# Expert tiles of two halves of 128 rows, each half with its own pair of experts

## What is computed

```
mod = (silu(c) @ wmod)                      # per sequence: sa, ca, ga, sb, cb, gb (ga, gb kept away from 0)
h = layernorm(x) * (1 + ca) + sa
x = x + ga * scan(h)                        # h_t = a_t * h_(t-1) + (1 - a_t) * v_t, times a sigmoid gate
h = layernorm(x) * (1 + cb) + sb
probs = softmax(h @ gate_w.T + gate_b)      # 8 experts
topk_vals, topk_idx = top_k(probs, 2)
y_e = relu(h @ w1[e] + b1[e]) @ w2[e] + b2[e]          # 128 -> 512 -> 128
x = x + gb * (topk_vals[0] * y_(first) + topk_vals[1] * y_(second))
```

## Time and profile before

| | us |
|---|---|
| median of 3 runs (lowest, highest) | 469.36 (467.02, 471.52) |
| the profiled execution | 468.58 |
| its span, from first to last instruction | 466.8 |
| mean granted TensorE clock, share of full | 0.923 |
| first stage, until the table is written | 0 to about 177 |
| expert tiles, first transposition to the end | 181.8 to 466.8 |

### The profile page before, as it was taken

One profiled execution on the slowest core, in us unless ns is written; L12 is line 12 of the kernel. 1 busy time (PEld: TensorE's weight loads), 2 busy tenths in 40 slices (PEclk: granted clock), 3 DMA queues, 4 the chain that ended last, 5 costly groups with the idle time before them and its releaser, 6 DMA issues.

```text
span 466.8 us, 14531 instructions
## 1 busy us (share of the span) xinstructions
PE 400.2 (86%) x4122; PEld 334.3 (72%) x4123; DVE 416.6 (89%) x1159; ACT 300.1 (64%) x746; POOL 214.4 (46%) x225
## 2 busy tenths in 40 slices
PE   1958888799888843998999999999999999999960
PEld 1434656456656742897999999999999988888960
DVE  4899999998989998987998999999999999999970
ACT  1447998787995610775767676677777666666630
POOL 8023330674775778854443444433333443333331
PEclk9997999978987555999999999999999999999995
DMA  7615534544223335442332333333333333222210
GB/s 228 187 47 190 164 127 117 178 144 148 104 85 121 129 147 160 161 132 68 104 107 65 102 99 82 101 86 86 82 85 89 85 82 82 82 67 77 67 44 15
DMA packets 47258, 50.51 MB, mean 108 GB/s; under 512 B 5342, under 2 KB 40879, under 8 KB 47202
## 3 DMA queue, kind: packets, MB, share of 16 engines
q1 hardware_dynamic: 39152, 32.64, 24.8%
q0 software_dynamic: 6976, 16.93, 10.0%
q10 hardware_dynamic: 1074, 0.23, 0.2%
HBM read 26.90 MB, written 24.57 MB: 110 GB/s over the span
## 4 chain that ended last, share of the span: by engine, by line
PE 55%; DVE 17%; issue 10%; POOL 9%; ACT 3%; DMA 3%; POOLq 1%; SPq 0%; ACTq 0%; DVEq 0%
POOL sorted_rows L562 9%; PE bank L1502 7%; PE bank L1519 7%; PE bank L1520 7%; PE bank L1522 7%; PE bank L1503 7%; PE bank L1504 7%; PE bank L1368 4%; DVE xn L922 3%; PE bank L1514 2%; PE bank L1488 2%; DVE st L860 2%; DVE hs L936 2%; DVE st L866 2%; DVE u L932 2%
## 5 line engine op out<-in xcount | busy, mean ns | idle before, releaser
L592 POOL DMA_INDIRECT out_dram<-tg,midx x90 | 103.0, 1145 | 151.3 <-DVE tg L1297 129.4
L756 ACT ACTIVATE xs<-bank,b1col 128x256 f32<-128x256 f32 x360 | 136.9, 488 | 26.2 <-PE bank L1504 20.9
L1519 PE MATMUL bank<-w2hi,xs 128*128 x720 | 119.2, 219 | 0.0
L1520 PE MATMUL bank<-w2hi,w2f 128*128 x720 | 119.0, 219 | 0.0
L1278 DVE TENSOR_TENSOR w2f<-xs 128x1024 f16<-128x1024 f32 x90 | 110.3, 1226 | 3.1
L1502 PE MATMUL bank<-xh,w1hi 128*128 128x256 f16 x360 | 98.8, 274 | 1.9 <-DVE xl L1269 1.9
L1522 PE MATMUL bank<-w2lo,xs 128*128 x720 | 98.9, 219 | 0.0
L1503 PE MATMUL bank<-xl,w1hi 128*128 128x256 f16 x360 | 98.7, 274 | 0.0
L1504 PE MATMUL bank<-xh,w1lo 128*128 128x256 f16 x360 | 98.6, 274 | 0.0
L562 POOL DMA_INDIRECT sorted_rows<-pay,idx x64 | 72.7, 1137 | 30.9 <-issue 18.8
L1520 PEld LDWEIGHTS bank<-w2hi,w2f 128*128 128x128 f16 x720 | 70.5, 98 | 0.8
(11 more groups left out here) (232 smaller groups left out, 671.2 us busy)
## 6 DMA issues: line engine op xcount, KB each, us to landing
xs<-sorted_rows SPq DMA_DIRECT2D x45, 260.0 KB, 2.8
sorted_rows<-padt SPq DMA_DIRECT2D x10, 582.0 KB, 5.2
xs<-sorted_rows SPq DMA_DIRECT2D x45, 128.0 KB, 2.5
w2f<-in_L_ffn_w_dram SPq DMA_DIRECT2D x4, 512.0 KB, 3.6
xs<-in_L_ffn_w_dram SPq DMA_DIRECT2D x4, 512.0 KB, 4.0
xs<-in_L_attn_x_dram SPq DMA_DIRECT2D x3, 512.0 KB, 8.5
out_dram<-tg,midx POOLq DMA_INDIRECT x90, 3.0
sorted_rows<-pay,idx POOLq DMA_INDIRECT x64, 2.7
```

Of the source, the lines that this page charges most:

```text
L592: pool.indirect_dma_start(out_rows, bass.IndirectOffsetOnAxis(midx[k][:, t:t + 1], 0), yout[k][:, t, :], None, bounds_check=TOK - 1, oob_i ...
L756: ins = act.activation(hf[e][:, cc, :], bank[2 * e + cc // 2][:, (cc % 2) * TW:(cc % 2 + 1) * TW], ACT.Relu, bias=b1col[:, bass.ds(ex[e] * ...
L1519: pe.matmul(o[t], hh[n % 2][e][:, cc, t * P:(t + 1) * P], whi, start=False, stop=False)
L1520: pe.matmul(o[t], hl[n % 2][e][:, cc, t * P:(t + 1) * P], whi, start=False, stop=False)
```

## The change

A tile is still 256 rows in two halves, but each half (a unit of `UNIT` = 128 rows) now has its own pair of experts. A pair with n tokens takes units of 128 rows, rounded up, and two units that follow each other in the table make a tile, whatever their experts are. The code of a tile holds four experts. DVE makes it from two table entries (`both_codes`), and PE and ACT wait for `codes_ready`. Layer 1 now runs by half (128 columns moving), `hidden` has 16 activations of 128x128, the bias of layer 2 is one matmul of 128 columns for each half and expert, and SP issues two DMAs for x and two for y, each with its own row number. The four weight arrays are cut into 16 tensors (one for each chunk of 128 hidden values, all experts in each), so that all addresses of an expert are one product plus a constant each. `addresses` has them worked out eight at a time before the matmuls of a half (nine with the bias). The padding takes 5 DMAs in place of 10; `drop`, `kept` and `row_mid` are half as large. The loads of w1 have runs of 512 B where they had 2 KB. Cut to its core:

```diff
-SPAN = TOK + TW
+UNIT = P
+SPAN = TOK + UNIT
-MAX_TURNS = (TOK // TW + PAIRS) // BUFS
+MAX_TURNS = (TOK // UNIT + PAIRS + 1) // (BUFS * HALVES)
...
-        w1hi = sb("w1hi", [P, E * H], F16)
-        w1lo = sb("w1lo", [P, E * H], F16)
-        w2hi = sb("w2hi", [P, E * H], F16)
-        w2lo = sb("w2lo", [P, E * H], F16)
+        w1hi, w1lo, w2hi, w2lo = ([sb(f"{n}{cc}", [P, E * D], F16) for cc in range(HC)]
+                                  for n in ("w1hi", "w1lo", "w2hi", "w2lo"))
...
-            return [code % E, code // E]
+            return [[code % E, code // E % E], [code // E ** 2 % E, code // E ** 3]]
...
             def load_x(it, k):
-                sp.dma_start(xin[k][:, :, :], tile_rows(it, k)[:, :, 0:D]).then_inc(x_tile_in[k], 16)
+                for t in range(HALVES):
+                    sp.dma_start(xin[k][:, t, :], unit_rows(it, k, t)[:, 0:D]).then_inc(x_tile_in[k], 16)
...
             def hidden(it, n, ex):
...
-                    for cc in range(HC):
-                        ins = act.activation(hf[e][:, cc, :], bank[2 * e + cc // 2][:, (cc % 2) * TW:(cc % 2 + 1) * TW],
-                                             ACT.Relu, bias=b1col[:, bass.ds(ex[e] * HC + cc, 1)])
+                    for t in range(HALVES):
+                        for cc in range(HC):
+                            o = cc % 2 * TW + t * P
+                            ins = act.activation(hf[e][:, cc, t * P:(t + 1) * P], bank[2 * e + cc // 2][:, o:o + P],
+                                                 ACT.Relu, bias=b1col[:, bass.ds(ex[t][e] * HC + cc, 1)])
...
-                done1 = marked(dve.tensor_tensor(cnti[:, 0:1], tend[:, PAIRS - 1:PAIRS], early_end[:, PAIRS - 1:PAIRS], ALU.add))
+                done1 = marked(dve.scalar_tensor_tensor(out=cnti[:, 0:1], in0=tend[:, PAIRS - 1:PAIRS], scalar=1.0,
+                                                        in1=early_end[:, PAIRS - 1:PAIRS], op0=ALU.add, op1=ALU.add))
...
-                done1 = marked(dve.tensor_scalar(cntt[:, 0:1], cnti[:, 0:1], BUFS.bit_length() - 1, None,
+                done1 = marked(dve.tensor_scalar(cntt[:, 0:1], cnti[:, 0:1], (BUFS * HALVES).bit_length() - 1, None,
                                                  ALU.arith_shift_right))
...
+            dve.wait_ge(table_ready, 1)
+            dve.scalar_tensor_tensor(out=both_codes[:, :], in0=bank[6][0:4, 1:P:2], scalar=float(E * E),
+                                     in1=table[:, 0:P:2], op0=ALU.mult, op1=ALU.add).then_inc(codes_ready, 1)
...
+            def addresses(expert, loaded, streamed=()):
+
+                for w in loaded:
+                    pe.to_reg(expert * D * 2 + (nc.lookup_mloc(w).addr + (P - 1) * 2))
+                for w in streamed:
+                    pe.to_reg(expert * D * 2 + nc.lookup_mloc(w).addr)
...
-                    for cc in range(HC):
-                        o = bank[2 * e + cc // 2][:, (cc % 2) * TW:(cc % 2 + 1) * TW]
-                        whi, wlo = (w[:, bass.ds(ex[e] * H + cc * P, P)] for w in (w1hi, w1lo))
-                        pe.matmul(o, whi, xh[n % 2][:, :], start=True, stop=False)
-                        pe.matmul(o, whi, xl[n % 2][:, :], start=False, stop=False)
-                        ins = pe.matmul(o, wlo, xh[n % 2][:, :], start=False, stop=True)
+                    for t in range(HALVES):
+                        addresses(ex[t][e], w1hi + w1lo)
+                        rows = slice(t * P, (t + 1) * P)
+                        for cc in range(HC):
+                            o = bank[2 * e + cc // 2][:, cc % 2 * TW + t * P:cc % 2 * TW + (t + 1) * P]
+                            whi, wlo = (w[cc][:, bass.ds(ex[t][e] * D, P)] for w in (w1hi, w1lo))
+                            pe.matmul(o, whi, xh[n % 2][:, rows], start=True, stop=False)
+                            pe.matmul(o, whi, xl[n % 2][:, rows], start=False, stop=False)
+                            ins = pe.matmul(o, wlo, xh[n % 2][:, rows], start=False, stop=True)
...
+                    for t in range(HALVES):
+                        addresses(ex[t][e], (), [b2row] + w2hi + w2lo)
+                        o = y_bank(n)[:, e * TD + t * D:e * TD + (t + 1) * D]
+                        rows = slice(t * P, (t + 1) * P)
+                        pe.matmul(o, ones16[:, :], b2row[:, bass.ds(ex[t][e] * D, D)], start=True, stop=False)
+                        for cc in range(HC):
+                            whi, wlo = (w[cc][:, bass.ds(ex[t][e] * D, D)] for w in (w2hi, w2lo))
+                            pe.matmul(o, hh[n % 2][e][:, cc, rows], whi, start=False, stop=False)
+                            pe.matmul(o, hl[n % 2][e][:, cc, rows], whi, start=False, stop=False)
+                            ins = pe.matmul(o, hh[n % 2][e][:, cc, rows], wlo, start=False, stop=cc == HC - 1)
...
-            held = [pe.alloc_register(f"held_expert{i}") for i in range(4)]
+            held = [pe.alloc_register(f"held_expert{i}") for i in range(8)]
```

More of the change, by code:

```diff
@@ L444, in settled @@
             def settled(n):
-                sp.wait_ge(landed, sp.value_load(table[2:3, n:n + 1], min_val=1, max_val=2))
+                last = n * HALVES + HALVES - 1
+                sp.wait_ge(landed, sp.value_load(table[2:3, last:last + 1], min_val=1, max_val=2))
                 sp.sem_inc(sp_turn, 1)
@@ L747, in experts_of @@
             def experts_of(it, n):
-                code = act.value_load(table[1:2, bass.ds(it * BUFS + n, 1)], min_val=0, max_val=E * E - 1)
-                return experts(act, code)
+                return experts(act.value_load(both_codes[1:2, bass.ds(it * BUFS + n, 1)], min_val=0, max_val=E ** 4 - 1))
             def hidden(it, n, ex):
@@ L1245, in tile_table @@
                 dve.wait_ge(dve_step, done)
[L1246 removed]
+                done = marked(dve.scalar_tensor_tensor(out=full[:, :], in0=sums[:, 2:3], scalar=-float(UNIT), in1=place[:, :],
                                                        op0=ALU.add, op1=ALU.min))
[L1248 removed]
+                mark(dve.scalar_tensor_tensor(out=over[:, :], in0=place[:, :], scalar=UNIT - (UNIT - 1) / 2, in1=sums[:, 2:3],
                                               op0=ALU.add, op1=ALU.subtract))
@@ L1259, in _ @@
             join()
-            dve.tensor_scalar(kept[:, :, :], row_mid[:, :, :], sums[:, 4:5], over[:, 0:1], ALU.mult, ALU.is_lt
+            dve.tensor_scalar(kept[:, :], row_mid[:, :], sums[:, 4:5], over[:, 0:1], ALU.mult, ALU.is_lt
                               ).then_inc(drop_made, 1)
@@ L1524, in layer2 @@
                 ins.then_inc(yps_ready, 1)
-            held = [pe.alloc_register(f"held_expert{i}") for i in range(4)]
+            held = [pe.alloc_register(f"held_expert{i}") for i in range(8)]
             def hold(before, now):
-                for reg, value in zip(held, before + now):
+                for reg, value in zip(held, [v for ex in (before, now) for half in ex for v in half]):
                     pe.reg_mov(reg, value)
             def held_experts():
-                b0, b1_, n0, n1 = (pe.snap(reg, min_val=0, max_val=E - 1) for reg in held)
-                return [b0, b1_], [n0, n1]
+                v = [pe.snap(reg, min_val=0, max_val=E - 1) for reg in held]
+                return [v[0:2], v[2:4]], [v[4:6], v[6:8]]
```

105 lines of the change are left out of this document (46 added, 59 removed).

## The result

The changed kernel takes 450.13 us (median of four runs, 448.51 to 452.80) against 468.19 us (465.48 to 471.52) of the kernel before on the same chip. The ratio is 0.9639, 95% interval 0.9596 to 0.9682. Its profiled execution has a span of 448.0 us (before 466.8), so 18.8 us are to be accounted for.

A forecast was written before the change was run, and what follows sets the result against it. PE was taken to stream columns without a gap in written-out tiles, losing about 0.25 us a tile in the loop. -36.0 + 2.7 + 2.8 + 3.1 + 1.3 = -26.1 us gave 443 us, range 432 to 463.

The forecast's parts named there:

- The tiles: Expert stage: 39 tiles for 45, all six taken from the hardware loop at 6.00 us each, 36.0 us saved.
- The array: PE, layer 1: 48 matmuls of 128 columns, 5.79 us a tile, 0.05 more; as slower-than-before rival, chance 0.02.
- The sequencer: PE's register work: +2.7 us in written-out tiles, +2.8 in the loop; as pace-setting rival 453 to 463 us, chance 0.14.
- the hole of 0.1 us ahead of layer 2: PE, written-out tiles: an issue wait before layer 2's first weight load, 0.1 us lost for each tile.
- a little more than that lead: PE's sequencer: hole between the layers becomes about 1.1 us, against a lead of about 1.0 us in steady tiles.
- The bound on this term: PE's sequencer: batches half as dear again (0.45 us) give 6.3 to 6.5 us for every tile, up to +19 us.
- the foretold lack of lead: Hardware loop: PE's sequencer has no lead there, 6.4 against 6.00 us on 7 intervals, +2.8 us.
- ACT: Sixteen activations take 4.3 us, hidden under 5.79 a tile, +1.3 at the end; as pace-setting rival, chance 0.06.
- The start: First tiles: more DMA issues by SP ahead of the third tile's x, +3.1 us.
- x comes 5 us later, and 1.9 of them aren't lost: Third tile's x lands about 5 us later, avoiding PE's old 1.94 us wait behind DVE: 5.0 - 1.9 = +3.1 us.
- wait of DVE near 212: Sign to look for: DVE's 4 us wait for the first written tile, until 212.46 before, is gone.
- The end: Last tile: nothing covers the lateness of ACT's activations, +1.3 us.

The follow-up runs named there:

- two traces of kernels that don't split the DMAs: Kernel before with layer 1 as 48 matmuls of 128 columns (ratio 1.0080); kernel before with 16 activations of 128x128 for 8 of 128x256 (1.0034).
- the other traces with this start: Changed kernel with 20 or 128 small matmuls, 18 turns, no read in the loop, or wide activations: 42.2 to 43.3 us from first to eighth transposition.
- the kernels with split DMAs: Kernel before with each x and y load issued as two DMAs of 128 rows: 472.71 us against 467.64, ratio 1.0152.
- ACT's halves: Kernel before with ACT's 8 activations of 128x256 a tile made 16 of 128x128: 468.78 us, ratio 1.0034.
- the version with both mended: Changed kernel with y loads of the first two tiles issued later and 20 small matmuls ahead of the tiles: 441.73 us, ratio 0.9412.

## Why the prediction was right, and where it was not

It gave 443 us in a range of 432 to 463; 450.13 lies in it, 7 us above the value.

**The tiles: right.** 39 of them, x loads in 78 parts, six intervals of 6.00 us fewer. It was the whole gain, and it came from counting units in the data and taking the price from the place where the tiles go, the loop.

**The array: right.** 0.056 us for a matmul of 128 columns in layer 1 too; the splitting alone costs 0.06 us a tile where 0.05 was said. A whole tile, 100 of them with two transpositions, takes 5.835 us.

**The sequencer: the mechanism right, one place wrong.** The batches are two packed instructions each, and taking them away costs 3.5 us a tile. But the hole of 0.1 us ahead of layer 2 in written-out tiles isn't there: "a little more than that lead" was a difference of two numbers about 1 us each. The interval grew by 0.09 all the same (5.745 to 5.835, steady), 0.06 from the split of layer 1, and 0.03 that no run here takes apart. So +2.3 for +2.7 is partly luck. The bound on this term was also added up too low: with batches half as dear again, eight of them put 1.2 us on the 5.1 to 6.0, which is up to 7.2 us a tile and not 6.5. It didn't come to that. In the loop the foretold lack of lead is what happens: the gap of 0.27 us ahead of each layer 2, from the read of the codes, and the back edge; 6.45 for 6.4.

**ACT: right in the tiles.** 4.23 us for the sixteen, 0.26 apart, 4.3 foretold, hidden behind PE. At the end it costs 0.5 to 1.4 us for the 1.3.

**The start: the step "x comes 5 us later, and 1.9 of them aren't lost" was mis-sized,** +3.1 for +6.4. That x of the third tile is late behind SP's eight issues was right: with four of them moved away the 4.9 us are back, and the third tile is 5.0 us later behind the first, as said. There is no wait of DVE near 212 and the interval with the stall is 2.2 us shorter, but this is in part luck: the stall is also missing from two traces of kernels that don't split the DMAs, so it wasn't a fixed cost of the kernel before that a later x could be counted on to remove. What failed is the overlap without a price: what the sum had no term for is that PE idles in these waits (3.54 us for the third x) and its clock falls behind them to 0.50, 2.5 us in the interval behind the third tile (1.3 to 1.4 in the other traces with this start). The clock in that stretch of the kernel before, where it had risen to 1.00 by 190, was not used. The rest of the miss is 0.9 us before the first transposition, which lies within what executions differ by, and the pace of the first intervals, which the sum left out, 0.3 us.

**The end: a cost that wasn't in the sum at all.** 1.3 of the 5.3 us were foretold (ACT's lateness), and with the code moved the end is 1.4 us longer than before. The other 3.9 are the hole behind the loop and the slow clock after it: the forecast had no term for PE's own code arriving late. Nothing in the rows of the kernel before shows such a hole. Its code has the end of a block 109 records behind the branch, and there two weight loads are 0.14 us apart, while in the kernels with split DMAs and with ACT's halves, whose PE code is the same, they are 0.69 and 0.83 us apart. A diff of the source doesn't tell where code lies in its block. It isn't a cost of this change's idea: 20 matmuls of no use take it away.

Taken together the two misses are 7.3 us, the distance from 443 to 450, and the version with both mended runs at 441.7.

## What to carry to other kernels

Price tiles that vanish at the place where they vanish, and check that the pace-setting engine really has the same pace in the new form; here that one row (0.056 us in layer 2) carried the forecast. Put several address sums of one base side by side: on this kernel that is the difference between 450 and 579 us. When DMAs are split, look at the first iterations, where no earlier tile hides them, and order them by when each is first waited for; and look at the first instructions behind a hardware loop in every new build, since here 20 small matmuls far ahead of it decided over a hole of 3 us there.

## What the runs showed of the hardware

- **Code behind a hardware loop stalled for 3 us** here, depending on where it lies. The same code has a gap of 3.0 us between two matmuls (2.8 and 3.3 in kernels with the same PE code), none when moved by 40 instructions, and 2.8 us when moved by 256. PE waits there for a fetch of 16 KB that begins 1.5 to 2.9 us behind the last branch and takes 0.9 to 1.5 us, and it goes on 1.2 to 1.6 us after that; with the 20 matmuls the block's end comes some 240 records behind the branch, and there is no wait. Why the fetch begins no earlier, and what the time behind it is, isn't shown. In the written-out tiles, with such a fetch for each 257 records, PE is busy 40.00 us of 40: there the fetches are hidden, and at the exit of this loop this one isn't.
- **Idling cost twice.** Behind the gap (3.04 us) and behind the wait for the third x (3.54 us) the granted clock is 0.50, and matmuls of 128 columns come 0.107 us apart rather than 0.056, for 3 us behind the gap and for 6 behind the wait for the third x. With PE kept busy in the first waits it was 0.96 to 1.00 there. Not every wait does it: behind one of 1.94 us it stayed at 1.00.
- **Single register instructions between the matmuls set PE's pace**: each lasts 32 ns, but three matmuls with two of them take 0.225 us, against 0.167 for three matmuls where the addresses are packed ahead of them, and a tile 3.5 us more.
